# Second gating cycle: layer 2 in three passes of split operands, and ACT's activations of layer 1 ahead of a turn's own

## What is computed

```python
def coupling_net(h):                       # 512 -> 512 -> 256 -> 128 -> 1
    h = gelu(h @ w1 + b1); h = gelu(h @ w2 + b2); h = gelu(h @ w3 + b3)
    return sigmoid(h @ w4 + b4)
def twist(x):
    o_r, o_i, p_r, p_i = split(x, 4)
    return concatenate([p_r, -p_i, -o_r, o_i])
out = layernorm(x)
for _ in range(3):                         # the three gating cycles
    tf = coupling_net(out)                 # one value per row
    combined = 0.7 * gf + 0.3 * tf         # gf: one value per batch, from a small net on the mean
    coupling = 0.1 + adaptive_range * (combined - 0.5) * 2.0
    out = out + coupling * twist(out)
x = x + tanh(g_ffn) * out
```

## Time and profile before

| | |
|---|---|
| median of 3 runs | 1707.92 us (1707.28 to 1707.93) |
| the profiled execution's own time | 1706.81 us |
| span of its trace, first to last instruction | 1705.0 us |
| mean granted clock of PE | 0.998 |
| busy: PE, DVE, ACT, POOL | 99%, 87%, 75%, 40% |
| the feed-forward phase | from about 1230 to 1705 us |

### The profile page before, as it was taken

How to read it: one execution, slowest core, us unless ns; L and a number is a source line. 1 busy time by engine, 2 the same in 40 slices (tenths; PEclk the granted TensorE clock), 3 DMA queues, 4 the chain that set the end, 5 groups by cost and what they waited for, 6 DMA issues and landing times. The chain is left out here.

```text
span 1705.0 us, 33568 instructions
## 1 busy us (share of the span) xinstructions
PE 1680.3 (99%) x12344; PEld 1283.1 (75%) x12344; DVE 1475.7 (87%) x2615; ACT 1272.9 (75%) x2249; POOL 680.1 (40%) x649
## 2 busy tenths in 40 slices
PE   8999999999999999999999999999999999999997
PEld 7888887777777777777777777777786685775864
DVE  6666666999999999999999999999788978969968
ACT  4233235999999999999999999999765576466556
POOL 3545443332388552586432785465323010100100
PEclk9999999999999999999999999999999999999999
DMA  9989966765477754667764675666515313412301
GB/s 317 355 309 333 340 248 177 170 168 135 140 190 183 142 140 107 149 204 143 162 150 121 150 198 128 142 134 154 182 35 160 91 50 99 139 50 52 113 26 50
DMA packets 165922, 270.09 MB, mean 158 GB/s; under 512 B 26736, under 2 KB 79216, under 8 KB 165760
## 3 DMA queue, kind: packets, MB, share of 16 engines
q1 hardware_dynamic: 110416, 158.84, 29.3%
q0 software_dynamic: 54768, 108.05, 27.0%
q10 hardware_dynamic: 576, 1.05, 0.2%
HBM read 179.48 MB, written 84.21 MB: 155 GB/s over the span
## 5 line engine op out<-in xcount | busy, mean ns | idle before, releaser
L1103 DVE CUSTOM_DVE_ANT_0 a_neg<-a_sc_ps,am 128x1024 f32<-128x1024 f32 x512 | 621.9, 1215 | 2.0 <-PE a_sc_ps L935 1.8
L1043 ACT ACTIVATE a_prob<-a_neg,a_row_min 128x1024 f32<-128x1024 f32 x512 | 585.6, 1144 | 14.7 <-DVE a_row_min L1103 8.6
L949 PEld LDWEIGHTS a_tr_ps<-ident,a_prob 128*128 128x128 f32 x4096 | 461.1, 140 | 89.2 <-issue 53.2
L949 PE MATMUL a_tr_ps<-ident,a_prob 128*128 128x128 f32 x4096 | 519.8, 274 | 0.9 <-ACT a_probT L1021 0.9
L1078 DVE COPY a_probT<-a_tr_ps 128x512 f32<-128x512 f32 x512 | 350.6, 685 | 36.9 <-PE a_tr_ps L949 35.3
L1021 ACT ACTIVATE a_probT<-a_tr_ps 128x512 f32<-128x512 f32 x512 | 303.8, 594 | 35.7 <-PE a_tr_ps L949 16.0
L831 POOL DMA_DIRECT2D a_q_st<-q_parts x144 | 79.5, 557 | 166.5 <-PE a_sc_ps L935 131.6
L935 PE MATMUL a_sc_ps<-k_first,a_q_st 96*128 96x512 f32 x384 | 126.3, 427 | 0.1
L935 PE MATMUL a_sc_ps<-a_k_st,a_q_st 96*128 96x512 f32 x384 | 126.0, 426 | 0.0
L969 PE MATMUL a_o_ps<-a_probT,a_v 128*32 128x256 f32 x2048 | 123.6, 382 | 0.6 <-ACT a_o L1032 0.6
L969 PE MATMUL a_o_ps<-a_probT,v_first 128*32 128x256 f32 x2048 | 123.8, 382 | 0.0
(11 more groups left out here) (246 smaller groups left out, 3299.7 us busy)
## 6 DMA issues: line engine op xcount, KB each, us to landing
a_q_st<-q_parts POOLq DMA_DIRECT2D x144, 128.0 KB, 3.9
k_first<-k_parts POOLq DMA_DIRECT2D x24, 512.0 KB, 8.4
a_k_st<-k_parts POOLq DMA_DIRECT2D x24, 512.0 KB, 7.6
a_m_raw<-mask SPq DMA_DIRECT2D x24, 512.0 KB, 4.9
a_adj_raw<-adj SPq DMA_DIRECT2D x24, 512.0 KB, 6.0
k_parts<-p_out_hi SPq DMA_DIRECT2D x32, 256.0 KB, 4.0
k_parts<-p_out_lo SPq DMA_DIRECT2D x32, 256.0 KB, 5.2
v_all<-p_v_out SPq DMA_DIRECT2D x8, 1024.0 KB, 4.8
```

Source lines behind the costliest of these rows:

```text
L949: last = pe.transpose(tr_ps[:, bank(u, half), j * P:(j + 1) * P], prob[:, r % NPROB, t * P:(t + 1) * P], ident[:])
L1043: act.activation(prob[:, r % NPROB, :], neg[:, r % 2, :], ACT.Exp, scale=-1.0, bias=row_min[:, r % 2:r % 2 + 1], accum_out=row_sum[:, r // ...
L1103: dve.tensor_tensor_reduce(out=neg[:, r % 2, :], in0=sc_ps[:, r % 2, :], in1=am[:, 2 * qb + qt, :], scale=-1.0, scalar=3.4e38, op0=ALU.add ...
```

## The change

In the second cycle layer 2 is split as in the other two: `SPLIT` becomes (0, 1, 2). ACT writes `u_hi_second` (fp32r) and `u_second` (f32) instead of the one `h1_second`; DVE has four more `split_u` per turn of the first cycle, between the tiles 0, 1 and 2, 3 of `turned`; PE makes three fp32r matmuls in place of one f32 matmul, with the weights `w2_kept`. PE's order of layers and turns is as it was. On ACT all eight activations of `h1` now stand ahead of the turn's `h2_half`, in turns 1 to 4. The buffers of the remainder lie where x rows and X of the next batch are loaded, so the load of the x rows' block 1 waits for layer 2 of turn 2 instead of turn 0, and POOL's first load for turn 3 instead of turn 1.

```diff
-    SPLIT = (0, 2)
+    SPLIT = (0, 1, 2)
...
-        h1_second = [nc.alloc_sbuf_tensor_at(f"f_h1_second{j}", [P, ET, CH], F32, offset=SB_AM + 8192 * j) for j in range(NJ)]
+        u_hi_second = [nc.alloc_sbuf_tensor_at(f"f_u_hi_second{j}", [P, ET, CH], F32R, offset=SB_AM + 8192 * j) for j in range(NJ)]
+        u_second = [nc.alloc_sbuf_tensor_at(f"f_u_second{j}", [P, ET, CH], F32, offset=u_hi_at[j]) for j in range(NJ)]
+        u_lo_second = [nc.alloc_sbuf_tensor_at(f"f_u_lo_second{j}", [P, ET, CH], F32R, offset=u_hi_at[j]) for j in range(NJ)]
...
                         if j == 1:
-                            sp.wait_ge(z2_ready, 2 * turn(b, 0, 0) + 2)
+                            sp.wait_ge(z2_ready, 2 * turn(b, 1, 0) + 2)
...
                 if j == 0:
-                    pool.wait_ge(z2_ready, 2 * turn(b - 1, 0, 1) + 2)
+                    pool.wait_ge(z2_ready, 2 * turn(b - 1, 1, 1) + 2)
...
                 for t in tiles:
-                    if n in SPLIT:
-                        pe.wait_ge(u_lo_ready, ET * turn_split(b, n, j) + t + 1)
-                    else:
-                        pe.wait_ge(h1_ready, ET * k + t + 1)
+                    pe.wait_ge(u_lo_ready, ET * turn_split(b, n, j) + t + 1)
                     for m in range(2):
                         ms = slice(m * P, (m + 1) * P)
-                        if n in SPLIT:
-                            last = three_pass(pe, acc[:, 2 * j + m, :], w_hi[:, t, ms], w_lo[:, t, ms], high[:, t, :], u_lo[j][:, t, :],
-                                              t == 0, t == ET - 1)
-                        else:
-                            last = pe.matmul(acc[:, 2 * j + m, :], w2[:, t, ms], h1_second[j][:, t, :], start=t == 0, stop=t == ET - 1)
+                        last = three_pass(pe, out[:, m, :], w_hi[:, t, ms], w_lo[:, t, ms], high[:, t, :], low_part[:, t, :],
+                                          t == 0, t == ET - 1)
...
                 for k in range(NJ * CYCLES):
                     n, j = k // NJ, k % NJ
-
-                    between = k > 0 and (k - 1) // NJ < CYCLES - 1
-                    other = (b, (k - 1) // NJ + 1, (k - 1) % NJ)
-                    def next_h1(*tiles):
-                        if between:
-                            for m in tiles:
-                                h1(*other, m)
-
-                    if k == 3:
-                        next_h1(0)
+                    if 1 <= k <= NJ * (CYCLES - 1):
+                        for m in range(ET):
+                            h1(b, (k - 1) // NJ + 1, (k - 1) % NJ, m)
                     h2_half(b, n, j, 0)
                     h2_half(b, n, j, 1)
...
                         second_cycle(b, j)
-                        turned(b, 0, ((0, 1, 2), (3,))[j])
-                        if j:
-                            turned(b, 1, (0, 1))
+                        turned(b, j, (0, 1))
+                        split_u(b, 1, j)
+                        turned(b, j, (2, 3))
                     elif n == 1:
                         third_cycle(b, j)
-                        if j == 0:
-                            turned(b, 1, (2,))
-                        split_u(b, 2, j, (1,))
-                        if j == 0:
-                            turned(b, 1, (3,))
-                        split_u(b, 2, j, (2, 3))
+                        split_u(b, 2, j, (1, 2, 3))
```

More of the change, by code:

```diff
@@ L1462, in layer2 @@
             def layer2(b, n, j, tiles):
-                k = turn(b, n, j)
+                out = acc[:, 2 * j:2 * j + 2]
                 if n == 0 and 0 in tiles:
@@ L1469, in layer2 @@
                         pe.wait_ge(shared_read, 4 * ET * NJ * (b + 1))
-                if n in SPLIT:
-                    pe.wait_ge(w2_lo_ready, b + 1)
-                    if n:
-                        pe.wait_ge(w2_kept_loaded, 32 * (b + 1))
+                pe.wait_ge(w2_lo_ready, b + 1)
+                if n:
+                    pe.wait_ge(w2_kept_loaded, 32 * (b + 1))
                 w_hi, w_lo = w2_kept if n else (w2_hi, w2_lo)
-                high = u_hi_third[j] if n else u_hi[j]
+                high = (u_hi, u_hi_second, u_hi_third)[n][j]
+                low_part = u_lo_second[j] if n == 1 else u_lo[j]
                 for t in tiles:
-                    if n in SPLIT:
-                        pe.wait_ge(u_lo_ready, ET * turn_split(b, n, j) + t + 1)
-                    else:
-                        pe.wait_ge(h1_ready, ET * k + t + 1)
+                    pe.wait_ge(u_lo_ready, ET * turn_split(b, n, j) + t + 1)
                     for m in range(2):
                         ms = slice(m * P, (m + 1) * P)
-                        if n in SPLIT:
-                            last = three_pass(pe, acc[:, 2 * j + m, :], w_hi[:, t, ms], w_lo[:, t, ms], high[:, t, :], u_lo[j][:, t, :],
-                                              t == 0, t == ET - 1)
-                        else:
-                            last = pe.matmul(acc[:, 2 * j + m, :], w2[:, t, ms], h1_second[j][:, t, :], start=t == 0, stop=t == ET - 1)
+                        last = three_pass(pe, out[:, m, :], w_hi[:, t, ms], w_lo[:, t, ms], high[:, t, :], low_part[:, t, :],
+                                          t == 0, t == ET - 1)
                         if t == ET - 1:
@@ L1621, in h1 @@
                 act.wait_ge(u_ready, ET * k + m + 1)
[L1622 to L1626, removed]
+                act.activation((u_hi_second if n == 1 else u_hi_third)[j][:, m, :], u[j][:, m, :], ACT.Gelu, bias=small.b1[:, m:m + 1])
+                act.activation((u_second if n == 1 else u)[j][:, m, :], u[j][:, m, :], ACT.Gelu, bias=small.b1[:, m:m + 1]).then_inc(h1_ready, 1)
             def h2_half(b, n, j, m):
@@ L1712, in batch @@
                         twist(b, 0, 2 if more else 1)
-                    next_h1(1 if k == 3 else 0)
                     h3_all(b, n, j)
@@ L1716, in batch @@
                         twist(b, 0, 3 if more else 2)
[L1717 to L1724, removed]
                     if n < CYCLES - 1:
@@ L1798, in split_u @@
                     dve.wait_ge(h1_ready, ET * turn(b, n, j) + m + 1)
-                    dve.tensor_tensor(u_lo[j][:, m, :], u[j][:, m, :], (u_hi_third if n else u_hi)[j][:, m, :].bitcast(F32), ALU.subtract).then_inc(u_lo_ready, 1)
+                    target, whole = (u_lo_second[j], u_second[j]) if n == 1 else (u_lo[j], u[j])
+                    dve.tensor_tensor(target[:, m, :], whole[:, m, :], (u_hi, u_hi_second, u_hi_third)[n][j][:, m, :].bitcast(F32), ALU.subtract).then_inc(u_lo_ready, 1)
             def in_turn(first, second):
```

## The result

| | before | after |
|---|---|---|
| median | 1707.6 us (1706.8 to 1707.9, 4 runs) | 1813.2 us (1805.8 to 1820.5, 4 runs) |
| profiled execution; its span | 1706.8; 1705.0 us | 1805.8; 1804.0 us |
| mean granted clock of PE | 0.998 | 0.974 |

The ratio is 1.062, 95% interval 1.057 to 1.067: 105.5 us slower. The direction was forecast. The size wasn't: 1786 was predicted, and the measured time lies 5 us above the range's upper end of 1808. The four executions after also lie 14.7 us apart, where those before lie within 1.1 us.

The account below looks back on a forecast made before the run. The prediction took PE, busy 99% of the span, to bound the kernel. It added 68.0 us of chain and 10.3 of clock to the profiled 1706.8, giving 1785.1 and a median of 1786, range 1771 to 1808.

Parts of the forecast that it names:

- The chain: ACT's order makes a batch's turns wait on one another in sequence: +16.99 us per batch, +68.0 for four.
- (a): From a turn's first `h2_half` (time H) to DVE's start: H + 6.64 us where beta is made.
- (b): Second cycle, from DVE's start (time D) through ACT's last `h1`: the next `h2_half` starts at D + 6.90 us.
- (e): First `h2_half` of turn 0 to turn 5: spacings 13.54, 13.54, 13.21, 13.21, 9.49, total 62.99 us against 46.00.
- No give-back between the batches: From one batch's turns to the next, PE stays the bound with unchanged work: at most 0.4 us a batch returned.
- DVE covered at 1.3 us a turn: DVE ends its 20 steps at D + 12.2, the next D is 13.54 later; its added 19.3 us are hidden.
- PE's 11.2 us: Less work from splitting layer 2 in 64 matmuls, forecast only to lengthen PE's wait for the next turn.
- The clock: PE's clock falls in half of 16 pauses, slowing three layer 3 records by 1.29 us each time: 10.3 us.
- A: Rival: the same chain in the turns, PE's clock holds; 1775.9 us, chance 0.27.
- B: Rival: the chain, and PE's clock falls nearly every time; up to 1839 us, more likely 1803, chance 0.09.
- C: Rival: ACT's order costs little, DVE bounds the turns and adds its 19.3 us; 1727 us, chance 0.04.
- D: Rival: ACT's eight activations finish before layer 2, nothing holds layer 3, PE's gain comes through; 1697 us, chance 0.03.

Follow-up runs that it names:

- e3: The changed kernel with 20 extra matmuls, whose sums nobody reads, in each of PE's 16 pauses; 1773.5 us, ratio 1.039.
- e4: The changed kernel without DVE's 32 second-cycle remainders, the third pass reading the high part instead; 1807.8 us, ratio 1.061.
- e10: e6 with both `h2_half` ahead of the first layer 1 activation in turn 3 too; 1724.2 us.
- e2: The changed kernel with ACT's order put back as in the kernel before, the split kept; 1789.2 us, ratio 1.048.
- e7: e6 with `turned` of block 1, eight operations per batch, moved from DVE to POOL; 1749.9 us, ratio 1.025.
- e5: e2 with the fourth activation of layer 1 moved ahead of the gate in turns 1 and 2; 1744.3 us, ratio 1.022.
- e1: The kernel before with only ACT's order changed, whole f32 layer 2 kept; 1795.6 us, ratio 1.052.
- e9: e1 with 12 extra matmuls in each of PE's 16 pauses; 1769.1 us, ratio 1.036.
- e6: e5 with DVE's first remainder right behind `second_cycle` and `turned` of block 1 behind `third_cycle` of block 0; 1725.4 us, ratio 1.011.

## Why the prediction was right in its mechanism and wrong in its size

- **The chain: right.** (a) H + 6.64 was 6.65 (1296.41 to 1303.06, where DVE starts), (b) D + 6.90 was 6.91 (to 1309.97). With the clock held in e3 all five spacings of (e) were met to 0.01.
- **No give-back between the batches: nearly.** 68.0 forecast, 66.7 measured in e3 against the kernel before on the same chip. The rest is the "at most 0.4 us a batch": from turn 5 to the next batch's turn 0 the changed kernel takes 69.21 us (1367.96 to 1437.17), the one before 69.64.
- **DVE covered at 1.3 us a turn, DMAs at nothing: right** (e4; the stretches and e3's sum leave no room for a transfer, and PE has no pause above 1 us in the turns but the 16).
- **PE's 11.2 us lost in a longer wait: right.** The sum without them meets e3's spacings to 0.01, and the pauses sum to 80.6 us.
- **The clock: the term that failed.** It was put at 10.3 us: a fall in 8 of 16 pauses, 1.29 us each. It was 39.7 us by the medians (32 in the profiled execution, 47 in the slowest, against e3). The trace shows both factors wrong. Every pause has its fall, 16 of 16. And a fall costs 1.6 to 2.7 us in batch 0 (1.5 to 3.0 in all four), not 1.29: all four records of layer 3 run at half speed (3.78 against 1.98, 1.8 us) and in some turns the tile behind them too. "Pauses longer than what came ahead of the only fall seen" had said it: with a pause of 5.2 us against 3.3, taking half of them had no row behind it. The bound that I had worked out, layer 3 at half speed 16 times, gives 1803, near the profiled 1805.8 and 10 below the median, but it only made the range's end (1808 with 0.3 us of error a turn) and not its middle; the other bound, 3.94 us a pause, was left out of the range.
- **Rivals.** A (clock holds) is what e3 measures: 1775.9 forecast, 1773.5 measured. B, whose likelier value was 1803, was the case that came, with 0.09. C and D are out by e4 and by ACT's rows. But C named its condition, `h2_half` not held, and where e10 meets it PE waits for DVE's remainders and the kernel is 17.9 us slower than before, near C's 19.3. How near is chance in part: C's sum let all of DVE's added work through and nothing of PE's gain.
- **The Trainium skill's rule** that the default state is throttled and activity releases it ("TensorE: Matmul & The Clock Gate", "What's actually happening"): the trace agrees, 0.50 to 0.54 over layer 3 behind each pause of batch 0, and full again behind the work of a turn. I named it beside the sum and sized the sum as if it held half the time.

## What to carry to other kernels

Where one queue serves two chains, work that depends on the last turn's result must not stand ahead of work that is already due: eight activations of 0.61 us ahead of two ready ones cost 4 us a turn here, and e2 shows the same on DVE with a single subtraction. Freeing one queue can bring the next one out: in e10 ACT holds nothing back, and PE waits for DVE's remainders. When a change makes PE pause for some microseconds, price the clock in every pause, with all that PE does first behind it at half speed; a filler of useless matmuls is a quick way to measure that part alone, and here recovered some 40 of 105.5 us. Before moving f32 elementwise work from DVE to an idle POOL, measure DVE's step while POOL runs, on the operands that it will have.

## What the runs showed of the hardware

**DVE and POOL can slow each other.** In e7, f32 tensor_tensor on 128x512 with all operands in SBUF, the on-chip memory of tiles: DVE 1.67 us from start to start beside POOL's, 0.60 alone; POOL's took 1.35 to 1.71 us, against 1.28 alone (L1378). It isn't so for every pair. Where one of DVE's two operands is a matmul sum (`f_acc`, in PSUM), DVE keeps 0.60 beside POOL, and POOL's two take 2.54 us together, 1.27 each. No run changes the place of the operand alone. Rows of e7:

```profile
1399.15 0.68 DVE L1786 TENSOR_TENSOR f_B<-f_B,f_acc 128x512 f32<-128x512 f32 x1
1399.50 2.54 POOL L1378 TENSOR_TENSOR f_pair_lo<-f_pair_raw,f_pair_hi 128x512 fp32r<-128x512 f32 x2 [14.34 <-ACT f_pair_hi L1598]
1399.75 0.68 DVE L1786 TENSOR_TENSOR f_A<-f_A,f_acc 128x512 f32<-128x512 f32 x1
```

**The length of a pause doesn't tell by itself whether the clock falls.** In e5 PE stood still 3.65 us and came back at full clock (in turn 1 of batch 0); in e1 it stood still 2.87 and in e9 2.14 us and came back at half. PE's rows: windows of e5, of e1 and of e9, first PE's pause, then the work behind it:

```profile
1308.00:1312.60 4.60, 0.95 (x4) 1.00 0.06 22
1312.60:1318.00 5.40, 5.40 (x23) 1.00 0.00 0
```

```profile
1321.50:1324.40 2.90, 0.09 (x1) 0.94 0.00 0
1324.46:1327.90 3.44, 3.44 (x5) 0.57 0.00 0
```

```profile
1346.40:1348.40 2.00, 0.00 (x0) 1.00 0.00 0
1348.49:1351.30 2.81, 2.81 (x5) 0.68 0.00 0
```

In e9 the clock was still full in the pause and fell behind its end. The same place in another batch of the same run can come out the other way: a fall comes in the pause or within 1.5 us behind it at e9's of 2.15 us in two batches of four, at e6's of 2.2 us in one of three, and at e5's of 3.65 us in turn 1 in three of four. Over all traces here, the turns show no fall at a pause of 1.8 us or less and one at every pause of 3.8 us or more; in the changed kernel's 16 pauses, 4.83 to 5.20 us long, it fell every time. What decides in between stays open.
